# Six layers of windowed attention on one core: another root, half of the normalisation on POOL, and the block transposes moved up

## The chip, the cores and the metric

The kernel runs on one core of one Trainium2 chip. The time is device microseconds from start to end. Three runs of the kernel before took 4267.52, 4268.81 and 4270.26 us; their median is 4268.81 us.

## The reference

The input is 8 batches of 512 tokens of width 128. It is normalised, and two branches take it: one full attention with 16 heads over each batch, and a stack of six layers of windowed attention and feed-forward. Their sum is added to the input. The change touches only the windowed attention of the six layers:

```python
def attn_layer(x, Wqkv, qs, ksc, Wo):
    q, k, v = split(x @ Wqkv)            # 16 heads of 64
    q = l2norm(q) * qs                   # t / max(norm(t), 1e-12)
    k = l2norm(k) * ksc
    q = q * cos * scale + rotate_half(q) * sin * scale
    k = k * cos / scale + rotate_half(k) * sin / scale
    out = local_attention(q, k, v)       # windows of 32: own and previous, softmax(8 q k)
    return out @ Wo
for i in range(6):
    x = attn_layer(shift_tokens(x), ...) + x
    x = ffn_layer(shift_tokens(x), ...) + x
```

## The kernel before, in words

There is no scheduler. Every engine has its own program, the order in it is the order in which the code is written, and engines wait for one another by semaphores. The full attention comes first; from about 1060 us on the layers run, and they are all that the change touches.

The layers go in **turns**. A turn handles one block of 128 tokens; four turns (c = 0 to 3) make a batch, eight batches a layer, so there are 192 turns with attention work, or 48 groups of four. The turns are pipelined over five stages: in one turn, TensorE projects the block that is four stages ahead, VectorE rotates the one three ahead, the scores of the one two ahead are computed, the softmax of the next one is finished, and the output of the present one is added to x. So one turn contains one of each of these on each engine, in this order:

- **DVE** (`turn` at L940): row sums of the exponentials `den` (L945) and reciprocal (L947), which wait for ACT's exponential; rotation of q, three multiplications with the tables (L897, L899), and the same for k; the sums of squares `ss` (L957), the maximum with a floor (L959), and a guess of the root by integer arithmetic (L961); in c = 0 the statistics of the feed-forward (L907 to L917); the addition to x (L968); the 32x32 block transposes `pT` (L972); a feed-forward gate (L924) or, in c = 1, a feed-forward addition (L980); the row maximum of the scores (L991) and their subtraction (L994); at last `qn`, rotated q and k times the root (L1001).
- **POOL**: softmax weights `pn` (L610), which wait for the reciprocal; the addition that ends the rotation of q (L614) and of k (L616); three steps of Newton's method for the root, four small instructions each (`newton`, L399); in c = 0 the same for the feed-forward with its normalisation (L625, L629).
- **ACT**: square of q (L722), copy of the transposed queries `qT` out of PSUM (L726), square of k (L729), copies of the transposed keys (L732, L733), gelu (L714), copy of `xT` (L749), the two copies of `y` (L706), the exponential (L759).
- **PE**: 8 transposes of q and 8 of k (L1042), the products with the output weights (L1254), feed-forward products, the transposed block (L1290), mask and scores (L1302, L1307), the **window products** (L1193), the projections of q and k (L1036).

Queries and keys have sums of squares for 32 heads in one tile `ss`, and one tile `rn` of roots. q is transposed into PSUM banks 0 and 1, k into banks 4 and 5. The products of L1254 go to bank 0 (`ps_o`), so they wait for the copy `qT`. The window products write banks 4, 5, 0 and 1; before them PE waits for `pT`, for the addition to x (which frees bank 0), for the copied keys and for `xT`:

```python
pe.wait_ge(l_pT, t + 2)
pe.wait_ge(l_xw[u], (s.l * NB + s.b + (2 if c == 3 else 1)) * 16)
past(pe, l_x, t + 1)
...
windows_times(u, (pool2, pool0)).then_inc(l_y, 1)
```

ACT's `y` copies wait for the window products, the exponential stands behind them in ACT's queue, and DVE's `den` of the next turn waits for the exponential.

Of the kernel before, what the change touches and what calls it, by code (L numbers as in the profile page):

```python
# [12 lines left out]
P = 128  # L13
# [25 lines left out]
NEG = -1e30  # L39
ROOT_CONSTS = (3.0, 12.0, 768.0)  # L40
ROOT_SCALE = 8192.0
RS = 11
RS_POOL = 12
STEPS = PAIRS * NU
NB_ = 8
# [42 lines left out]
def build(nc, x_in, consts, a_logit, a_bout, a_wqk, a_wv, a_wo, l_wqk, l_wv, l_wo, l_scale, l_w1, l_w2, l_small, out, xd, accd, vd):  # L88
# [8 lines left out]
    with ExitStack() as ctx:  # L97
# [44 lines left out]
        c15 = sb("c15", [P, 2 * H])  # L142
        root_const = sb("root_const", [P, len(ROOT_CONSTS), 2 * H])
        floor_const = sb("floor_const", [P, 2 * H])
        rn = sb("rn", [P, 2 * H])
        rt = sb("rt", [P, 2 * H])
# [84 lines left out]
        l_fl = sem("l_fl")  # L231
        l_gs = sem("l_gs")
        l_rs = sem("l_rs")
# [54 lines left out]
        l_rotk = sem("l_rotk")  # L288
        l_qn = sem("l_qn")
        l_tq = sem("l_tq")  # L290
        l_tk = sem("l_tk")
# [96 lines left out]

        def newton(pool, done, count, root, half, tmp, steps=range(RS_POOL), scaled=False):

            for step in steps:
                const = root_const[:, step // 4] if scaled else c15[:, 0:root.shape[-1]]
                to, a, b, op = ((tmp, root, root, ALU.mult), (tmp, tmp, half, ALU.mult),
                                (tmp, const, tmp, ALU.subtract), (root, root, tmp, ALU.mult))[step % 4]
                if step:
                    pool.wait_ge(done, count * RS_POOL + step)
                nc.gpsimd.tensor_tensor(to, a, b, op).then_inc(done, 1)  # L399

        block = ctx.enter_context(nc.Block())
# [150 lines left out]
        def _(pool):  # L552
            nc.gpsimd.memset(zero[:], 0.0).then_inc(s_zero, 1)
            nc.gpsimd.memset(c15[:], 1.5).then_inc(s_avg, 1)
            for k, value in enumerate(ROOT_CONSTS):
                nc.gpsimd.memset(root_const[:, k], value).then_inc(s_avg, 1)
            nc.gpsimd.memset(floor_const[:], NORM_FLOOR).then_inc(s_avg, 1)
            nc.gpsimd.memset(ones, 1.0).then_inc(s_avg, 1)
            pool.wait_ge(s_avg, 3 + len(ROOT_CONSTS))

# [44 lines left out]
            def turn(s):  # L605
# [6 lines left out]
                if s.has(3):  # L612
                    pool.wait_ge(l_rq, t + 4)
                    nc.gpsimd.tensor_tensor(t1[:, 0:INNER], t1[:, 0:INNER], t2[:, 0:INNER], ALU.add).then_inc(l_rotq, 1)  # L614
                    pool.wait_ge(l_rk, t + 4)
                    nc.gpsimd.tensor_tensor(t1[:, INNER:2 * INNER], t1[:, INNER:2 * INNER], t2[:, INNER:2 * INNER],  # L616
                                            ALU.add).then_inc(l_rotk, 1)
                    pool.wait_ge(l_gs, t + 4)
                    newton(pool, l_rs, t + 3, rn[:], ss[:], rt[:], scaled=True)
                if c == 0 and s.ffn(1):  # L620
# [15 lines left out]
        def _(act):  # L636
# [80 lines left out]
            def turn(s):  # L717
# [5 lines left out]
                if s.has(2):  # L723
                    act.wait_ge(l_tq, t + 3)
                    past(act, l_s, t + 2)
                    act.activation(qT[:].rearrange("p h c -> p (h c)"), pool0, ACT.Copy).then_inc(l_qT, 1)  # L726
                if s.has(3):
# [38 lines left out]
        def _(dve):  # L766
# [174 lines left out]
            def turn(s):  # L941
# [27 lines left out]
                if s.has(1):  # L969
                    dve.wait_ge(l_p, t + 2)  # L970
                    past(dve, l_y, t + 1)
                    nc.vector.transpose(pT[:].rearrange("p n h q -> p n h q"),  # L972
                                        pn[:].rearrange("p (h n k) -> p n h k", h=H, n=2)).then_inc(l_pT, 1)
                if c == 0 and s.ffn(2):
# [31 lines left out]
            dve.wait_ge(s_avg, 3 + len(ROOT_CONSTS))  # L1006
            layers(dve, turn)


        @block.tensor  # L1010
        def _(pe):
# [27 lines left out]

            def transposes(i, pool, src):  # L1040
                for a in range(PAIRS):
                    t = nc.tensor.transpose(pool[:, a * P:(a + 1) * P], src[:, i * INNER + a * P:i * INNER + (a + 1) * P], ident)  # L1042
                return t
# [190 lines left out]
            def turn(s):  # L1234
                c, t = s.c, s.t
                part = fold_part(s)
                if s.has(2):
                    pe.wait_ge(l_qn, t + 3)
                    past(pe, l_y1sb, t + 1)
                    if s.has(3):  # L1240
                        past(pe, l_xT, t + 4)
                    transposes(0, pool0, qn[:]).then_inc(l_tq, 1)
                    past(pe, l_y0sb, t + 1)
                    transposes(1, pool2, qn[:]).then_inc(l_tk, 1)
                if s.has(0):
# [10 lines left out]
                if part is not None:  # L1256
                    n, v, q = part
                    if s.has(2):
                        pe.wait_ge(l_qT, t + 3)
                    past(pe, l_xT, t + 4)  # L1260
                    fold(n, q)
                if s.turn_of(1, 1):
                    pe.wait_ge(l_qT, t + 3)
                    ffn_bias(s.l)
# [15 lines left out]
                if s.has(4):  # L1280
                    pe.wait_ge(l_xs[c], (s.l * NB + s.b + 2) * 16)
                    if s.has(2):
                        pe.wait_ge(l_qT, t + 3)
                    past(pe, l_xT, t + 4)
# [6 lines left out]
                if s.has(2):  # L1291
# [4 lines left out]
                    else:  # L1296
                        past(pe, l_sub, t + 2)
                    pe.wait_ge(l_qT, t + 3)
                    pe.wait_ge(l_kT, t + 3)
# [132 lines left out]
```

## Time and profile before

| | us |
|---|---|
| median of three runs | 4268.81 |
| the profiled execution | 4268.13 |
| its span | 4266.1 |
| PE busy | 3952.3 (93%) |
| DVE busy | 3893.6 (91%) |
| POOL busy | 2675.2 (63%) |
| ACT busy | 2604.4 (61%) |

The span is what lies between the first and the last instruction of the profile; some 2 us lie around it. Busy shares are means over stages: the full attention up to about 1060 us, the layers up to about 4200 us, and an end of some 66 us in which the pipeline drains. In the rows further down, a line of the timeline gives the start, the duration, the engine, the line of the code, the operation, output and inputs, and in brackets how long the engine stood idle before it and who ended that.

### The profile page before, as it was taken

What the parts mean: (1) busy time and instruction counts of PE and PEld (TensorE: products, weight loads), DVE (VectorE), ACT (ScalarE), POOL (GpSimd) and SP (SyncE); (2) the same over time, 40 slices, a digit from 0 to 9 for tenths busy, and PEclk for the clock granted to TensorE, in tenths of its full rate; (3) what the DMA queues carried; (4) which work ended last, traced back from release to release, by engine and by line L of the source; (5) the groups of instructions that cost most, each with busy time, mean ns of one, the idle gap of its engine ahead of it and who ended that gap; (6) DMA issues with size and microseconds to landing.
All of it is one profiled execution on the core that took longest, in us unless ns stands there. A gap on an engine that the chain in (4) does not pass through costs nothing. (4 is left out here: it accounts for less than half of the span.)

```text
span 4266.1 us, 124858 instructions
## 1 busy us (share of the span) xinstructions
PE 3952.3 (93%) x48616; PEld 2743.1 (64%) x48616; DVE 3893.6 (91%) x4860; ACT 2604.4 (61%) x3780; POOL 2675.2 (63%) x4692
## 2 busy tenths in 40 slices
PE   7999999996899999999999999999999999999996
PEld 4666666664666666666666666666666666666664
DVE  6888888886999999999999999999999999999994
ACT  4555565563566666666666666666666666666663
POOL 5555555554676766767667676666766767667673
PEclk9999999998999999999999999999999999999999
DMA  5444444441000011000110001100011000010000
GB/s 134 92 92 94 94 94 91 91 93 45 23 16 17 16 30 29 16 17 16 30 29 16 17 16 30 30 16 17 16 29 29 16 17 16 20 38 16 18 15 14
DMA packets 342439, 165.07 MB, mean 39 GB/s; under 512 B 114240, under 2 KB 337472, under 8 KB 341184
## 3 DMA queue, kind: packets, MB, share of 16 engines
q1 hardware_dynamic: 342208, 161.99, 17.1%
q8 instruction: 145, 2.38, 0.2%
q14 instruction: 86, 0.70, 0.1%
HBM read 115.67 MB, written 33.69 MB: 35 GB/s over the span
## 5 line engine op out<-in xcount | busy, mean ns | idle before, releaser
L610 POOL TENSOR_TENSOR pn<-es,rden 128x1024 f32<-128x1024 f32 x192 | 366.3, 1908 | 693.6 <-DVE rden L947 693.6
L706 ACT ACTIVATE y<-ps 128x1024 f32<-128x1024 f32 x384 | 372.2, 1021 | 510.2 <-PE ps L1193 510.2
L614 POOL TENSOR_TENSOR t<-t 128x1024 f32<-128x1024 f32 x192 | 454.3, 2366 | 88.0 <-DVE t L899 88.0
L658 ACT ACTIVATE t<-ps,amx 128x512 f32<-128x512 f32 x512 | 347.6, 688 | 250.9 <-DVE amx L805 250.9
L899 DVE TENSOR_TENSOR t<-ps,tabl 128x512 f32<-128x512 f32 x768 | 490.8, 681 | 0.0
L897 DVE TENSOR_TENSOR t<-ps,tabl 128x1024 f32<-128x1024 f32 x384 | 467.0, 1216 | 16.7 <-ACT sq L722 11.4
L616 POOL TENSOR_TENSOR t<-t 128x1024 f32<-128x1024 f32 x192 | 452.6, 2357 | 3.6 <-DVE t L899 3.6
L1001 DVE TENSOR_TENSOR qn<-t,rn 128x2048 f32<-128x2048 f32 x192 | 438.1, 2282 | 5.1 <-POOL rn L399 5.1
L957 DVE TENSOR_REDUCE ss<-sq 128x32 f32<-128x2048 f32 x192 | 436.9, 2275 | 0.0
L805 DVE TENSOR_REDUCE amx<-ps 128x2 f32<-128x1024 f32 x256 | 310.9, 1215 | 129.5 <-PE ps L1064 129.5
L1042 PEld LDWEIGHTS ps<-cst,qn 128*128 128x128 f32 x3072 | 349.3, 141 | 116.0 <-issue 59.9
L1254 PE MATMUL ps<-acc,y 128*128 128x128 f32 x3072 | 367.9, 278 | 36.9 <-ACT qT L726 32.6
L1254 PE MATMUL ps<-wm,y 128*128 128x128 f32 x3072 | 365.7, 277 | 33.8 <-ACT qT L726 33.8
L1254 PEld LDWEIGHTS ps<-acc,y 128*128 128x128 f32 x3072 | 352.5, 193 | 58.0 <-issue 57.9
L1307 PE MATMUL ps<-kpad,qT 128*32 128x128 f32 x12288 | 385.5, 279 | 0.0
L1254 PEld LDWEIGHTS ps<-wm,y 128*128 128x128 f32 x3072 | 350.2, 192 | 53.9 <-issue 53.9
L1042 PE MATMUL ps<-cst,qn 128*128 128x128 f32 x3072 | 370.0, 274 | 13.1 <-DVE qn L1001 10.3
L1036 PE MATMUL ps<-wm,xT 128*128 128x512 f32 x768 | 357.9, 609 | 8.8 <-ACT xT L749 8.8
L1307 PEld LDWEIGHTS ps<-kpad,qT 128*32 128x32 f32 x12288 | 332.0, 112 | 45.6 <-issue 44.2
L1036 PE MATMUL ps<-acc,xT 128*128 128x512 f32 x768 | 355.2, 605 | 0.0
L813 DVE STREAM_TRANSPOSE kpad<-t 128x1024 f32<-128x1024 f32 x256 | 315.4, 1232 | 0.0
L1064 PE MATMUL ps<-qk 64*128 64x512 f32 x1024 | 291.4, 646 | 4.3 <-ACT t L658 3.5
(134 smaller groups left out, 8234.2 us busy)
## 6 DMA issues: line engine op xcount, KB each, us to landing
wm<-values_dram SPq DMA_DIRECT2D x128, 256.0 KB, 5.2
y<-values_dram SPq DMA_DIRECT2D x128, 256.0 KB, 4.9
values_dram<-qT SPq DMA_DIRECT2D x64, 256.0 KB, 2.3
tokens_dram<-x SPq DMA_DIRECT2D x96, 128.0 KB
xs<-tokens_dram SPq DMA_DIRECT2D x192, 64.0 KB, 1.8
xw<-tokens_dram SPq DMA_DIRECT2D x192, 64.0 KB, 1.9
xsh<-x SPq DMA_DIRECT2D x48, 128.0 KB
xsh<-x SPq DMA_DIRECT2D x48, 127.0 KB
```

Source lines behind the costliest of these rows:

```text
L610: nc.gpsimd.tensor_tensor(heads(pn[:], H), heads(es[:], H), rden[:].unsqueeze(2).to_broadcast([P, H, KEYS]), ALU.mult).then_inc(l_p, 1)
L614: nc.gpsimd.tensor_tensor(t1[:, 0:INNER], t1[:, 0:INNER], t2[:, 0:INNER], ALU.add).then_inc(l_rotq, 1)
L616: nc.gpsimd.tensor_tensor(t1[:, INNER:2 * INNER], t1[:, INNER:2 * INNER], t2[:, INNER:2 * INNER], ALU.add).then_inc(l_rotk, 1)
L706: return act.activation(y[:].rearrange("p h (w q) -> p w h q", w=NW)[:, 2 * half:2 * half + 2], src.rearrange("p (w h q) -> p w h q", w=2, ...
L897: nc.vector.tensor_tensor(t13, q3, tabl[:, 0, u, i].unsqueeze(1).to_broadcast([P, H, DH]), ALU.mult)
L899: sine = nc.vector.tensor_tensor(t23[:, :, lo:lo + DH // 2], q3[:, :, hi:hi + DH // 2], tabl[:, 1, u, i, lo:lo + DH // 2].unsqueeze(1).to_ ...
L957: nc.vector.tensor_reduce(ss[:], heads(sq[:], 2 * H), X, ALU.add).then_inc(l_ss, 1)
L1001: nc.vector.tensor_tensor(heads(qn[:], 2 * H), heads(t1, 2 * H), rn[:].unsqueeze(2).to_broadcast([P, 2 * H, DH]), ALU.mult).then_inc(l_qn, 1)
L1036: m = nc.tensor.matmul(pool[:, s * 512:(s + 1) * 512], src, wqkL[v][:, i * INNER + s * 512:i * INNER + (s + 1) * 512], start=True, stop=True)
L1042: t = nc.tensor.transpose(pool[:, a * P:(a + 1) * P], src[:, i * INNER + a * P:i * INNER + (a + 1) * P], ident)
L1254: m = nc.tensor.matmul(ps_o, y[:, h], mhL[s.v][:, slot(h)], start=(h == 0), stop=(h == H - 1))
L1307: m = nc.tensor.matmul(pool1[w * WIN:(w + 1) * WIN, a * 2 * KEYS:(a + 1) * 2 * KEYS], qT[:, a, w * WIN:(w + 1) * WIN], kpad[:, 2 * a:2 * a ...
```

## The change

In each turn of the layers:

1. The root. The guess on DVE (L961) and the three Newton steps on POOL are replaced by one instruction of POOL that raises the floored sum of squares to the power -0.5, and one Newton step of four instructions behind it (`polish`), all on 128x32 elements. The constants follow: the tables are now divided by 2, not by 8192.
2. The normalisation. DVE multiplies only the query half by its root (128x1024 in place of 128x2048); the key half is a POOL instruction, behind the root in POOL's queue, with a semaphore `l_kn` of its own, for which PE's transposes of k wait.
3. The query copy. PE signals the transposes of q in two halves, one for each PSUM bank, and ACT copies them in two instructions of 128x512; PE's output products wait for the first, what comes later for the second.
4. The order on DVE. The block transposes `pT` stand ahead of the sums of squares, and no longer behind the addition to x.

```diff
-ROOT_CONSTS = (3.0, 12.0, 768.0)
-ROOT_SCALE = 8192.0
+ROOT_CONST = 3.0
+ROOT_SCALE = 2.0
...
+        def polish(pool, done, count, root, square, const, tmp):
+            nc.gpsimd.tensor_tensor(root, square, power_const[:, 0:root.shape[-1]], ALU.pow).then_inc(done, 1)
+            pool.wait_ge(done, count * RS_STEP + 1)
+            nc.gpsimd.tensor_tensor(tmp, root, root, ALU.mult).then_inc(done, 1)
+            pool.wait_ge(done, count * RS_STEP + 2)
+            nc.gpsimd.tensor_tensor(tmp, tmp, square, ALU.mult).then_inc(done, 1)
+            pool.wait_ge(done, count * RS_STEP + 3)
+            nc.gpsimd.tensor_tensor(tmp, const, tmp, ALU.subtract).then_inc(done, 1)
+            pool.wait_ge(done, count * RS_STEP + 4)
+            nc.gpsimd.tensor_tensor(root, root, tmp, ALU.mult).then_inc(done, 1)
...
@@ POOL, turn
-                    pool.wait_ge(l_gs, t + 4)
-                    newton(pool, l_rs, t + 3, rn[:], ss[:], rt[:], scaled=True)
+                    pool.wait_ge(l_fl, t + 4)
+                    polish(pool, l_rs, t + 3, rn[:], ss[:], root_const[:], rt[:])
+                if s.has(3):
+                    pool.wait_ge(l_rotk, t + 4)
+                    pool.wait_ge(l_rs, (t + 4) * RS_STEP)
+                    past(pool, l_tk, t + 3)
+                    nc.gpsimd.tensor_tensor(heads(qn[:, INNER:2 * INNER], H), heads(t1[:, INNER:2 * INNER], H),
+                                            rn[:, H:2 * H].unsqueeze(2).to_broadcast([P, H, DH]), ALU.mult).then_inc(l_kn, 1)
@@ ACT, turn
-                    act.wait_ge(l_tq, t + 3)
                     past(act, l_s, t + 2)
-                    act.activation(qT[:].rearrange("p h c -> p (h c)"), pool0, ACT.Copy).then_inc(l_qT, 1)
+                    for half in range(2):
+                        act.wait_ge(l_tq, 2 * t + 5 + half)
+                        act.activation(qT[:, 4 * half:4 * half + 4].rearrange("p h c -> p (h c)"), bank(half),
+                                       ACT.Copy).then_inc(l_qT, 1)
@@ DVE, turn
+                    past(dve, l_kn, t + 3)
                     rotate(1, u, pool1, l_rk)
+                if s.has(1):
+                    dve.wait_ge(l_p, t + 2)
+                    past(dve, l_y, t + 1)
+                    nc.vector.transpose(pT[:].rearrange("p n h q -> p n h q"),
+                                        pn[:].rearrange("p (h n k) -> p n h k", h=H, n=2)).then_inc(l_pT, 1)
+                if s.has(3):
                     nc.vector.tensor_reduce(ss[:], heads(sq[:], 2 * H), X, ALU.add).then_inc(l_ss, 1)
                     dve.wait_ge(l_ss, t + 4)
                     nc.vector.tensor_tensor(ss[:], ss[:], floor_const[:], ALU.max).then_inc(l_fl, 1)
-                    dve.wait_ge(l_fl, t + 4)
-                    nc.vector.tensor_scalar(rn[:].bitcast(I32), ss[:].bitcast(I32), -0.5, float(0x5F3759DF),
-                                            ALU.mult, ALU.add).then_inc(l_gs, 1)
...
-                    dve.wait_ge(l_rs, (t + 4) * RS_POOL)
+                    dve.wait_ge(l_rs, (t + 4) * RS_STEP)
                     dve.wait_ge(l_rotq, t + 4)
-                    dve.wait_ge(l_rotk, t + 4)
-                    past(dve, l_tk, t + 3)
-                    nc.vector.tensor_tensor(heads(qn[:], 2 * H), heads(t1, 2 * H),
-                                            rn[:].unsqueeze(2).to_broadcast([P, 2 * H, DH]), ALU.mult).then_inc(l_qn, 1)
+                    past(dve, l_tq, 2 * t + 6)
+                    nc.vector.tensor_tensor(heads(qn[:, 0:INNER], H), heads(t1[:, 0:INNER], H),
+                                            rn[:, 0:H].unsqueeze(2).to_broadcast([P, H, DH]), ALU.mult).then_inc(l_qn, 1)
@@ PE, turn
-                    transposes(0, pool0, qn[:]).then_inc(l_tq, 1)
+                    for half in range(2):
+                        transposes(0, pool0, qn[:], half).then_inc(l_tq, 1)
+                    pe.wait_ge(l_kn, t + 3)
                     past(pe, l_y0sb, t + 1)
                     transposes(1, pool2, qn[:]).then_inc(l_tk, 1)
...
-                        pe.wait_ge(l_qT, t + 3)
+                        pe.wait_ge(l_qT, 2 * t + 5)
```

DVE before, one turn (c = 2) from `den` to the gate; the line numbers are those of each kernel:

```order
L945 TENSOR_REDUCE den<-es 128x16
L947 RECIPROCAL rden<-den 128x16
L897 TENSOR_TENSOR t<-ps,tabl 128x1024
L899 TENSOR_TENSOR t<-ps,tabl 128x16x32 x2
L897 TENSOR_TENSOR t<-ps,tabl 128x1024
L899 TENSOR_TENSOR t<-ps,tabl 128x16x32 x2
L957 TENSOR_REDUCE ss<-sq 128x32
L959 TENSOR_TENSOR ss<-ss,floor_const 128x32
L961 TENSOR_SCALAR rn<-ss 128x32
L968 TENSOR_TENSOR x<-x,ps 128x128
L972 STREAM_TRANSPOSE pT<-pn 128x1024
L924 SCALAR_TENSOR_TENSOR fh<-ps,b1s,qk 128x512
```

DVE now, the same turn:

```order
L967 TENSOR_REDUCE den<-es 128x16
L969 RECIPROCAL rden<-den 128x16
L919 TENSOR_TENSOR t<-ps,tabl 128x1024
L921 TENSOR_TENSOR t<-ps,tabl 128x16x32 x2
L919 TENSOR_TENSOR t<-ps,tabl 128x1024
L921 TENSOR_TENSOR t<-ps,tabl 128x16x32 x2
L983 STREAM_TRANSPOSE pT<-pn 128x1024
L986 TENSOR_REDUCE ss<-sq 128x32
L988 TENSOR_TENSOR ss<-ss,floor_const 128x32
L994 TENSOR_TENSOR x<-x,ps 128x128
L946 SCALAR_TENSOR_TENSOR fh<-ps,b1s,qk 128x512
```

`pT` has moved up past the sums, the floor and the addition to x; the guess is gone; the addition to x is now the last of the two things of DVE that the window products wait for.

POOL before, from the key rotation on (`rn` is the root, `rt` its temporary); eleven more such small instructions follow the first one shown, eight of them left out here:

```order
L616 TENSOR_TENSOR t<-t 128x1024
L399 TENSOR_TENSOR rt<-rn 128x32
L398 ISA
L399 TENSOR_TENSOR rt<-rt,ss 128x32
L398 REGISTER_ALU
L399 TENSOR_TENSOR rt<-root_const,rt 128x32
L398 REGISTER_ALU
L399 TENSOR_TENSOR rn<-rn,rt 128x32
L398 REGISTER_ALU
```

POOL now, the same place:

```order
L630 TENSOR_TENSOR t<-t 128x1024
L405 TENSOR_TENSOR rn<-ss,power_const 128x32
L406 REGISTER_ALU
L407 TENSOR_TENSOR rt<-rn 128x32
L408 REGISTER_ALU
L409 TENSOR_TENSOR rt<-rt,ss 128x32
L410 REGISTER_ALU
L411 TENSOR_TENSOR rt<-root_const,rt 128x32
L412 REGISTER_ALU
L413 TENSOR_TENSOR rn<-rn,rt 128x32
L636 REGISTER_ALU
L638 TENSOR_TENSOR qn<-t,rn 128x1024
```

Five small instructions stand where twelve stood, and the key half of `qn` has come in behind them.

## Rows read from the trace of the kernel before

**Rows 1.** Busy time by engine over the layers (span, then busy, clock, DMA).

```profile
1060.00:4200.00 3140.00, 2965.47 (x28343) 2056.47 (x28342) 3031.95 (x3774) 1999.21 (x2318) 2112.52 (x3493) 1.00 0.08 21
```

**Rows 2.** Waits over 1095 to 4200 us: total, times, longest.

```profile
PE ps L1193 <- DVE pT L972: 73.8, 54, 1.7
PE ps L1254 <- ACT qT L726: 65.3, 186, 0.5
```

**Rows 3.** Timeline of PE: window products of c=0 and c=1, turn c=2, next c=0.

```profile
2998.04 1.14 PE L1193 MATMUL ps<-pT,xw 32*128 32x512 f32 x8 [1.74 <-DVE pT L972]
...
3014.92 1.14 PE L1193 MATMUL ps<-pT,xw 32*128 32x512 f32 x8
...
3020.39 1.91 PE L1042 MATMUL ps<-cst,qn 128*128 128x128 f32 x16
3022.64 3.81 PE L1254 MATMUL ps<-acc,y 128*128 128x128 f32 x32 [0.33 <-ACT qT L726]
...
3030.41 1.14 PE L1193 MATMUL ps<-pT,xw 32*128 32x512 f32 x8
...
3063.20 1.14 PE L1193 MATMUL ps<-pT,xw 32*128 32x512 f32 x8 [1.68 <-DVE pT L972]
```

**Rows 4.** Timeline of ACT in turn c=2, and its 512-wide copy in c=1.

```profile
3010.03 0.60 ACT L743 ACTIVATE qk<-ps 128x512 f32<-128x512 f32 x1 [1.58 <-PE ps L1202]
...
3016.99 1.94 ACT L706 ACTIVATE y<-ps 128x1024 f32<-128x1024 f32 x2 [3.89 <-PE ps L1193]
3018.81 1.06 ACT L759 ACTIVATE es<-es 128x1024 f32<-128x1024 f32 x1
```

**Rows 5.** Timeline of DVE in turn c=2, to the next turn's `den`.

```profile
3019.91 1.22 DVE L945 TENSOR_REDUCE den<-es 128x16 f32<-128x1024 f32 x1 [0.16 <-ACT es L759]
...
3026.00 2.27 DVE L957 TENSOR_REDUCE ss<-sq 128x32 f32<-128x2048 f32 x1
3028.30 0.27 DVE L959 TENSOR_TENSOR ss<-ss,floor_const 128x32 f32<-128x32 f32 x1
3028.61 0.18 DVE L961 TENSOR_SCALAR rn<-ss 128x32 int32<-128x32 int32 x1
3028.74 0.29 DVE L968 TENSOR_TENSOR x<-x,ps 128x128 f32 x1
3028.94 1.24 DVE L972 STREAM_TRANSPOSE pT<-pn 128x1024 f32<-128x1024 f32 x1
...
3033.12 2.28 DVE L1001 TENSOR_TENSOR qn<-t,rn 128x2048 f32<-128x2048 f32 x1
3035.39 1.22 DVE L945 TENSOR_REDUCE den<-es 128x16 f32<-128x1024 f32 x1
```

**Rows 6.** Timeline of DVE in turn c=0: the statistics and the transposes.

```profile
3059.69 0.87 DVE L907 BATCH_NORM_STATS2 st<-xsh 128x6 f32<-128x128 f32 x4
...
3061.63 1.24 DVE L972 STREAM_TRANSPOSE pT<-pn 128x1024 f32<-128x1024 f32 x1
```

**Rows 7.** Timeline of POOL in turn c=2: weights, key rotation, first and last Newton instruction.

```profile
3021.49 1.90 POOL L610 TENSOR_TENSOR pn<-es,rden 128x1024 f32<-128x1024 f32 x1 [4.84 <-DVE rden L947]
...
3026.16 2.37 POOL L616 TENSOR_TENSOR t<-t 128x1024 f32<-128x1024 f32 x1
3028.87 0.24 POOL L399 TENSOR_TENSOR rt<-rn 128x32 f32<-128x32 f32 x1 [0.34 <-DVE rn L961]
...
3032.46 0.25 POOL L399 TENSOR_TENSOR rn<-rn,rt 128x32 f32<-128x32 f32 x1
```

**Rows 8.** Timeline of DVE: the floor in c=1, the normalisation in c=0.

```profile
3011.50 1.01 DVE L959 TENSOR_TENSOR ss<-ss,floor_const 128x32 f32<-128x32 f32 x1
...
3065.81 2.28 DVE L1001 TENSOR_TENSOR qn<-t,rn 128x2048 f32<-128x2048 f32 x1
```

**Rows 9.** Timeline of POOL, same places: key rotation, and a feed-forward Newton instruction.

```profile
3010.10 2.36 POOL L616 TENSOR_TENSOR t<-t 128x1024 f32<-128x1024 f32 x1
...
3065.86 2.28 POOL L399 TENSOR_TENSOR frt<-frn 128x4 f32<-128x4 f32 x1
```

More of the change, by code:

```diff
@@ L39 @@
 NEG = -1e30
-ROOT_CONSTS = (3.0, 12.0, 768.0)
-ROOT_SCALE = 8192.0
+ROOT_CONST = 3.0
+ROOT_SCALE = 2.0
 RS = 11
 RS_POOL = 12
+RS_STEP = 5
 STEPS = PAIRS * NU
@@ L142, in build @@
         c15 = sb("c15", [P, 2 * H])
-        root_const = sb("root_const", [P, len(ROOT_CONSTS), 2 * H])
+        root_const = sb("root_const", [P, 2 * H])
         floor_const = sb("floor_const", [P, 2 * H])
+        power_const = sb("power_const", [P, 2 * H])
         rn = sb("rn", [P, 2 * H])
@@ L231, in build @@
         l_fl = sem("l_fl")
-        l_gs = sem("l_gs")
         l_rs = sem("l_rs")
@@ L289, in build @@
         l_qn = sem("l_qn")
+        l_kn = sem("l_kn")
         l_tq = sem("l_tq")
@@ L387, in heads, with newton @@
             return ap.rearrange("p (h d) -> p h d", h=n)
-        def newton(pool, done, count, root, half, tmp, steps=range(RS_POOL), scaled=False):
+        def newton(pool, done, count, root, half, tmp, steps=range(RS_POOL)):
             for step in steps:
-                const = root_const[:, step // 4] if scaled else c15[:, 0:root.shape[-1]]
                 to, a, b, op = ((tmp, root, root, ALU.mult), (tmp, tmp, half, ALU.mult),
-                                (tmp, const, tmp, ALU.subtract), (root, root, tmp, ALU.mult))[step % 4]
+                                (tmp, c15[:, 0:root.shape[-1]], tmp, ALU.subtract), (root, root, tmp, ALU.mult))[step % 4]
                 if step:
@@ L554, in _ @@
             nc.gpsimd.memset(c15[:], 1.5).then_inc(s_avg, 1)
-            for k, value in enumerate(ROOT_CONSTS):
-                nc.gpsimd.memset(root_const[:, k], value).then_inc(s_avg, 1)
+            nc.gpsimd.memset(root_const[:], ROOT_CONST).then_inc(s_avg, 1)
             nc.gpsimd.memset(floor_const[:], NORM_FLOOR).then_inc(s_avg, 1)
+            nc.gpsimd.memset(power_const[:], -0.5).then_inc(s_avg, 1)
             nc.gpsimd.memset(ones, 1.0).then_inc(s_avg, 1)
-            pool.wait_ge(s_avg, 3 + len(ROOT_CONSTS))
+            pool.wait_ge(s_avg, 5)
             def copy_batch(b):
@@ L968, in turn @@
                     nc.vector.tensor_tensor(xb, xb, ps_o, ALU.add).then_inc(l_x, 1)
[L969 to L973, printed above, removed]
                 if c == 0 and s.ffn(2):
@@ L996, in turn @@
                 if s.has(3):
-                    dve.wait_ge(l_rs, (t + 4) * RS_POOL)
+                    dve.wait_ge(l_rs, (t + 4) * RS_STEP)
                     dve.wait_ge(l_rotq, t + 4)
-                    dve.wait_ge(l_rotk, t + 4)
-                    past(dve, l_tk, t + 3)
-                    nc.vector.tensor_tensor(heads(qn[:], 2 * H), heads(t1, 2 * H),
-                                            rn[:].unsqueeze(2).to_broadcast([P, 2 * H, DH]), ALU.mult).then_inc(l_qn, 1)
+                    past(dve, l_tq, 2 * t + 6)
+                    nc.vector.tensor_tensor(heads(qn[:, 0:INNER], H), heads(t1[:, 0:INNER], H),
+                                            rn[:, 0:H].unsqueeze(2).to_broadcast([P, H, DH]), ALU.mult).then_inc(l_qn, 1)
             dve.wait_ge(s_tb, 16)
             scale_tables(0)
-            dve.wait_ge(s_avg, 3 + len(ROOT_CONSTS))
+            dve.wait_ge(s_avg, 5)
             layers(dve, turn)
@@ L1038, in project, with transposes @@
                 return m
-            def transposes(i, pool, src):
-                for a in range(PAIRS):
+            def transposes(i, pool, src, half=None):
+                for a in range(PAIRS) if half is None else range(half * 4, half * 4 + 4):
                     t = nc.tensor.transpose(pool[:, a * P:(a + 1) * P], src[:, i * INNER + a * P:i * INNER + (a + 1) * P], ident)
@@ L1258, in turn @@
                     if s.has(2):
-                        pe.wait_ge(l_qT, t + 3)
+                        pe.wait_ge(l_qT, 2 * t + 6)
                     past(pe, l_xT, t + 4)
@@ L1262, in turn @@
                 if s.turn_of(1, 1):
-                    pe.wait_ge(l_qT, t + 3)
+                    pe.wait_ge(l_qT, 2 * t + 6)
                     ffn_bias(s.l)
@@ L1282, in turn @@
                     if s.has(2):
-                        pe.wait_ge(l_qT, t + 3)
+                        pe.wait_ge(l_qT, 2 * t + 6)
                     past(pe, l_xT, t + 4)
@@ L1297, in turn @@
                         past(pe, l_sub, t + 2)
-                    pe.wait_ge(l_qT, t + 3)
+                    pe.wait_ge(l_qT, 2 * t + 6)
                     pe.wait_ge(l_kT, t + 3)
```

## The prediction

> **What bounds the kernel now.** I read the busy table first. Over the layers PE is busy 2965 of 3140 us (94%) and DVE 3032 (97%), POOL 2113 and ACT 1999 [rows 1]. Two engines are nearly full, so shares alone don't say what a lighter DVE is worth; the order of waits within a turn must. The waits view is short: PE waits 74 us for the block transposes, 54 times, and 65 us for the query copy, 186 times at 0.35 [rows 2].
>
> Then I followed one group of four turns in the timeline. I call the start of the window products W. From W of one c=0 turn to W of the next, 3063.20 - 2998.04 = 65.16 us [rows 3]; 48 groups make 3128 us, which is the layers' 3140. Single turns: c=1 takes 16.88, c=2 15.49 [rows 3], c=3 (no row, the same instructions as c=2) 15.5, and c=0 the rest, 17.3.
>
> Three chains have nearly one length there. *PE's own*: in c=1 and c=2 it has only the 0.33 us before L1254 to spare, in c=0 also the 1.68 for the transposes [rows 3]. *DVE's own*: its rows of c=2 stand back to back, from `den` at 3019.91 to `den` at 3035.39, 15.48 us [rows 5]. *The ring through all engines*: W at 3014.92, the copies of y at 3016.99, the exponential to 3019.87, `den` at 3019.91 (0.16 idle, released by the exponential), and along DVE to the end of pT at 3030.18, then W at 3030.41 [rows 3 to 5]. Shortening DVE alone therefore leaves the ring: W to `den` is 4.99 us of PE and ACT that the change doesn't touch.
>
> **The change part by part.**
>
> *Half of `qn` leaves DVE.* 2.28 us for 2048 elements become about 1.2 for 1024 (half, plus some start; the half-sized rows on DVE, such as `den`, have 1.22) [rows 5]. DVE loses 1.1 us a turn. In the ring this is worth nothing: the end of `qn` and the end of the exponential release `den` at the same moment now (3035.40 and the 0.04 behind the exponential), so DVE will stand 1.1 us waiting for the exponential instead. 192 turns take some 200 us off DVE's busy time and leave the end where it is.
>
> *The guess goes.* From the floor to the next instruction there are 28.74 - 28.30 = 0.44 us in c=2, of which the guess with its wait is 0.18 to 0.31 [rows 5]; I take the lower, its own duration. This lies in the ring, in every turn.
>
> *The transposes move up.* pT starts 2.9 us earlier. But the window products wait for the addition to x too, and this now stands behind the sums, the floor and (in c=0) the statistics, where pT stood. DVE has the same work between `den` and the later of the two: in c=2 the last releaser ended at 3030.18 [rows 5] and will end at 3030.18 - 0.18 = 3030.00. What ends last has another name; the time is that of the guess. The hand-over from DVE to W was 0.33 us in c=0, where PE stood waiting (61.63 + 1.24 = 62.87, then 63.20) [rows 3, 6]; behind an addition it could be none or the same 0.35. I take 0.2, since part of the waits that follow pT's in PE's program is then already past. So W of c=2 comes at 3030.20 in place of 3030.41, 0.21 earlier; c=3 the same; c=0 at 62.87 - 0.18 + 0.2 = 62.89 in place of 63.20, 0.31 earlier. The hand-over's ends, 0 and 0.35, make each of the three 0.2 better or 0.15 worse.
>
> *The query copy by banks.* L1254 starts 2.25 us behind the transposes' start, and these take 1.91 [rows 3]: 0.33 of wait. In future the first bank is transposed after 0.5 us, its copy takes about 0.60 [rows 4], and is there before the transposes of k are through. In c=1, where PE is the longest chain, 0.33 come off: W to W 16.55. DVE's ring in c=1 is 15.3, so it doesn't hold this back. In the other turns PE's own chain becomes 15.15, just below the ring. ACT pays 0.17 a turn for two starts instead of one; it has idle time in each turn, and its next piece, the square of k, starts no later.
>
> *The root.* Of twelve instructions from 3028.87 to 3032.71, 0.33 apart [rows 7], five are left: p for the power and 4 x 0.33 = 1.3. No row shows a power on POOL. Its nearest row is a multiplication of the same shape, 0.24 [rows 7]; the other end is the dearest instruction that POOL has here, 2.36 [rows 9], and beyond it the whole old chain, 3.8. I take 0.25 to 0.85, near the first, because up to 0.85 it makes no difference, as follows. The Trainium skill (GPSIMD Engine Reference, section "Performance versus the Vector engine") gives a cost of about 12 cycles an element for branches on the data; for 32 elements at the page's 1.2 GHz that is an estimate of 0.32 us on top of the multiplication's time. No run here shows it.
>
> *The key half on POOL.* The form is that of `pn`, 1.90 [rows 7]; POOL is idle 4.84 us in front of the next `pn`, and the root gets 2.5 us shorter less p. In c=2 the addition to x now ends at 3030.0 and begins at 3029.7, where the floor ends; the power starts 0.1 later, the root is ready at 3031.1 + p and the key product runs from 3031.2 + p to 3033.1 + p. PE's transposes of k need it at 3036.6: free. But DVE wants to start the query half at 3033.12 - 0.18 = 3032.94, and here is a cover to look at. Two rows show that DVE and POOL exclude each other in instructions with two inputs from SBUF: the floor in c=1 took 1.01 us in place of 0.27 and ended as the key rotation ended (3012.51 and 3012.46), and a POOL instruction of 0.20 took 2.28 beside `qn` [rows 8, 9]. So the query half waits for the key half, until 3033.1 + p, and `den` can follow 1.2 later, at 3034.3 + p. The exponential lets it start at 3035.18: there are 0.85 us of cover for p. In c=1 turns the sums are done 1.2 us earlier relative to W, in c=0 turns the root has the 1.74 us of the statistics; only the intervals behind c=2 and c=3 are exposed. The feed-forward's root in c=0, behind it on POOL, starts some 0.9 + p later but is held by a `qn` half as long; it stays within 0.5 us of where it was, and `pn` with it.
> The Trainium skill (SBUF — State Buffer, section "Who interferes with whom") says the same of such pairs: whichever starts first keeps the shared read port for its whole instruction and the other blocks. The trace agrees, with the 2.28 for 0.20.
>
> *Sum.* 0.33 (c=1) + 0.21 + 0.21 + 0.31 = 1.06 us a group, 48 groups: 51 us. From the profiled execution's 4268.1 that gives 4217; the median of the runs is 0.7 above it, within their spread. With the hand-over's ends, 3 x 0.2 or 3 x 0.15 x 48, own range 4190 to 4240.
>
> **The rivals.**
>
> *B, PE becomes the only bound.* If the early pT freed the window products, PE would lose all four 0.33 and the 1.68: 65.16 - 3.0 = 62.2 a group, 144 us, 4124. For it speaks that the waits view names pT alone. Against it: the addition to x is a wait of the same instruction, and DVE reaches it no earlier.
>
> *C, a middling power.* For p between 0.85 and 1.7 the key half is in front of the query half each time, and the two exposed turns of a group lose p - 0.85 each: 96 us for each us. At p = 1.3 that is 43 of the 51 us back, 4260.
>
> *D, slower: POOL holds the read port in front of the query half.* The same place, with the point of decision p = 0.85 + 51/96 = 1.4. At p = 2.36 [rows 9] c=2 and c=3 lose 1.5 each, c=1's early sums no longer suffice (0.35), and `pn` with both rotations come late enough in c=1 to hold the floor (0.3): 3.65 lost, 1.06 won, 124 us, 4392. For it: a power is more than a multiplication, and POOL is the slower engine for the same shape already (2.36 for an addition of 128x1024 [rows 9], where DVE takes half of 2.28 for a product of that size). Against it: nothing in the trace; only that the query half could win the start from p = 1.7 on, since both wait for the same root. Then nearly all of the gain stays, 4230.
>
> *E, no change.* If the addition's hand-over is 0.35 and the guess was hidden by PE's own 15.15 plus new waits (for the key half, between the transposes), c=2 and c=3 give nothing and c=0 and c=1 little: 4262 to 4275.
>
> **How the numbers follow.** Forecast 0.53; B 0.04; C 0.17, of which 0.10 is still faster by over 0.2% (9 us, about what a measurement of this kernel can tell from no change), 0.03 within it and 0.04 slower; D 0.18, with 0.03 in the branch that stays faster and 0.15 slower; E 0.08, 0.05 within 0.2% and 0.03 slower. Faster 0.70, same 0.08, slower 0.22. The range goes from the forecast's own lower end, 4190, up to 4290, where p is 1.6; outside lie B and most of D.
>
> **What would show it.** Right: DVE's busy time falls to about 3620 us, with an idle of about 1 us in front of `den` for the exponential; W follows the addition to x, not pT; PE has no wait left before L1254's successor; a group of four turns takes 64.1 us, with 15.3 in c=2 and c=3, 17.0 in c=0 and 16.55 in c=1; the power takes under 0.85. Wrong: a query half that starts when the key half ends and pushes `den` past the exponential (C, D), or a PE without idle in c=0 (B).

## The result, and the profile after

The changed kernel takes 4915.24 us (median of four runs, 4910.09 to 4917.95) where the kernel before took 4268.17 in the same comparison: a ratio of 1.151, 95% interval 1.149 to 1.153. The prediction said 4217, with a range of 4190 to 4290. It had the wrong sign.

The page of the changed kernel names the reason in its first group: the power on POOL takes 5.44 us, 192 times. That is 1044 us of POOL's time. Its line:

```profile
L405 POOL TENSOR_TENSOR rn<-ss,power_const 128x32 f32<-128x32 f32 x192 | 1044.4, 5440 | 176.0 <-DVE ss L988 169.9
```

The waits from 1100 to 4800 us (total, times, longest) answer to [rows 2]:

```profile
DVE qn L1021 <- POOL rn L413: 495.6, 179, 4.3
PE ps L1062 <- DVE qn L1021: 477.9, 174, 4.0
...
DVE pT L983 <- POOL pn L624: 54.3, 42, 3.0
...
PE ps L1213 <- DVE x L994: 46.0, 48, 1.5
```

In this stretch DVE waits for the root 179 times, and PE waits for DVE's query half 174 times. DVE's `den` waited for ACT's exponential in only 7 of the 192 turns, 7.6 us together, so neither PE nor ACT stands in the chain that now sets the turn. The query copy is no longer among PE's waits, and the window products wait for the addition to x where they waited for pT. The busy row over the layers, the answer to [rows 1], has PE at 84%, DVE at 81% and POOL at 82%: none of them is full. DVE and POOL wait for each other in turn, and PE waits for DVE. The mean granted clock of TensorE over this stretch is 0.94, where it was 1.00:

```profile
1100.00:4840.00 3740.00, 3132.39 (x28030) 2203.14 (x28029) 3044.88 (x3556) 2013.77 (x2486) 3051.99 (x2328) 0.94 0.07 17
```

One turn (c = 2) on DVE, the answer to [rows 5]:

```profile
3501.66 1.21 DVE L967 TENSOR_REDUCE den<-es 128x16 f32<-128x1024 f32 x1
...
3507.74 1.24 DVE L983 STREAM_TRANSPOSE pT<-pn 128x1024 f32<-128x1024 f32 x1
3508.90 2.24 DVE L986 TENSOR_REDUCE ss<-sq 128x32 f32<-128x2048 f32 x1
3511.18 0.19 DVE L988 TENSOR_TENSOR ss<-ss,floor_const 128x32 f32<-128x32 f32 x1
3511.31 0.29 DVE L994 TENSOR_TENSOR x<-x,ps 128x128 f32 x1
...
3514.06 1.23 DVE L1015 TENSOR_TENSOR es<-ps,mx 128x1024 f32<-128x1024 f32 x1
3518.34 2.92 DVE L1021 TENSOR_TENSOR qn<-t,rn 128x1024 f32<-128x1024 f32 x1 [3.06 <-POOL rn L413]
3521.18 1.21 DVE L967 TENSOR_REDUCE den<-es 128x16 f32<-128x1024 f32 x1
```

and on POOL, the answer to [rows 7]:

```profile
3511.45 5.44 POOL L405 TENSOR_TENSOR rn<-ss,power_const 128x32 f32<-128x32 f32 x1 [1.18 <-DVE ss L988]
3516.97 0.24 POOL L407 TENSOR_TENSOR rt<-rn 128x32 f32<-128x32 f32 x1
...
3517.95 0.25 POOL L413 TENSOR_TENSOR rn<-rn,rt 128x32 f32<-128x32 f32 x1
3518.28 1.90 POOL L638 TENSOR_TENSOR qn<-t,rn 128x1024 f32<-128x1024 f32 x1
```

Read the two together and the turn closes on itself: 9.71 us from `den` to the end of the floor, 5.60 for the power with its hand-overs, 1.31 for the polishing, 1.90 in which POOL has the key half and DVE's query half, issued 0.06 later, is blocked, and 1.00 until `den` starts again. That is 19.52 us, where the turn took 15.48 [rows 5]. The query half alone takes 1.22 us (a run below shows it); here it shows as 2.92, because the time in which it is blocked counts as its own.

POOL is not always the first. In 22 of the 192 turns DVE started 0.10 us ahead, and there it is the key half on POOL that is blocked:

```profile
1687.03 1.23 DVE L1021 TENSOR_TENSOR qn<-t,rn 128x1024 f32<-128x1024 f32 x1 [3.35 <-POOL rn L413]
1687.12 2.89 POOL L638 TENSOR_TENSOR qn<-t,rn 128x1024 f32<-128x1024 f32 x1
```

This turn (c=3, with the same work as the one above) took 17.65 us where the others take 19.52, and so did nearly all of the 22. In 164 turns POOL was ahead by 0.05 to 0.08 us; what decides between the two was not found. In the last 6, all c=1, DVE reached its half 0.6 to 1.9 us behind POOL.

The turn c=1 takes 2.26 us more than c=2. The feed-forward work of POOL stands between the key half of c=0 and the softmax weights of c=1, so the transposes wait for the weights, and the key rotation, late by as much, holds DVE's floor for 1.02 us:

```profile
3487.19 1.25 DVE L983 STREAM_TRANSPOSE pT<-pn 128x1024 f32<-128x1024 f32 x1 [1.14 <-POOL pn L624]
...
3490.64 1.21 DVE L988 TENSOR_TENSOR ss<-ss,floor_const 128x32 f32<-128x32 f32 x1
```

The starts of `den` in all 192 turns give the account by turn (median us from one `den` to the next; the last column is the mean over all 191 intervals):

| kernel | c=0 | c=1 | c=2 | c=3 | mean |
|---|---|---|---|---|---|
| before | 17.38 | 16.81 | 15.48 | 15.48 | 16.59 |
| after | 19.54 | 21.78 | 19.52 | 19.52 | 19.95 |
| after, multiplication for the power | 16.84 | 16.24 | 15.27 | 15.27 | 16.15 |
| after, key half behind | 17.83 | 22.22 | 17.81 | 17.81 | 19.02 |
| after, transposes back | 18.47 | 21.58 | 18.45 | 18.45 | 19.10 |
| the best version below | 15.99 | 16.58 | 15.24 | 14.92 | 15.96 |

191 intervals times 3.36 are 642 us; the medians of the runs differ by 647. So nearly the whole loss lies in the turns.

PE's part, the answer to [rows 3]:

```profile
3501.80 3.33 PE L1062 MATMUL ps<-cst,qn 128*128 128x128 f32 x16 [3.59 <-DVE qn L1021]
3504.96 3.74 PE L1276 MATMUL ps<-acc,y 128*128 128x128 f32 x32
...
3512.66 1.14 PE L1213 MATMUL ps<-pT,xw 32*128 32x512 f32 x8
```

The sixteen transposes take 3.33 us where they took 1.91. PE had just stood 3.59 us, and the granted clock was at the lower of its two levels, 1.2 of 2.4 GHz, while they ran:

```profile
3501.50:3504.50 3.00, 2.70 (x13) 2.71 (x14) 2.96 (x5) 1.29 (x3) 1.26 (x1) 0.50 0.00 0
```

This is a consequence and no further cause in these turns: DVE had the scores, had subtracted their maximum and still stood 3.06 us before it got its root.

### The profile page after: what moved, and what is told of

Read it like the earlier page. It is cut to its first block and busy times, and to the rows that moved or that the text cites. A ratio compares the mean times of both kernels' runs of the same rounds, so it can differ in the third digit from the quotient of the medians.

```text
span 4913.3 us, 123751 instructions
## 1 busy us (share of the span) xinstructions
PE 4155.9 (85%) x48616; PEld 2915.8 (59%) x48616; DVE 3927.9 (80%) x4668; ACT 2637.6 (54%) x3972; POOL 3671.7 (75%) x3539
## 5 line engine op out<-in xcount | busy, mean ns | idle before, releaser
L405 POOL TENSOR_TENSOR rn<-ss,power_const 128x32 f32<-128x32 f32 x192 | 1044.4, 5440 | 176.0 <-DVE ss L988 169.9
L1062 PE MATMUL ps<-cst,qn 128*128 128x128 f32 x3072 | 511.7, 335 | 516.1 <-DVE qn L1021 504.5
L1021 DVE TENSOR_TENSOR qn<-t,rn 128x1024 f32<-128x1024 f32 x192 | 516.7, 2691 | 523.9 <-POOL rn L413 523.9
L1062 PEld LDWEIGHTS ps<-cst,qn 128*128 128x128 f32 x3072 | 448.4, 174 | 677.3 <-DVE qn L1021 504.6
L747 ACT ACTIVATE qT<-ps 128x512 f32<-128x512 f32 x384 | 217.0, 596 | 626.1 <-PE ps L1062 625.4
L638 POOL TENSOR_TENSOR qn<-t,rn 128x1024 f32<-128x1024 f32 x192 | 386.8, 2015 | 16.3
L1276 PE MATMUL ps<-acc,y 128*128 128x128 f32 x3072 | 390.8, 290 | 4.3 <-ACT y L726 4.3
L1276 PE MATMUL ps<-wm,y 128*128 128x128 f32 x3072 | 390.9, 290 | 0.0
L1276 PEld LDWEIGHTS ps<-acc,y 128*128 128x128 f32 x3072 | 386.9, 208 | 5.9 <-issue 5.9
L1276 PEld LDWEIGHTS ps<-wm,y 128*128 128x128 f32 x3072 | 387.2, 208 | 0.0
```

Source lines behind the costliest of these rows:

```text
L405: nc.gpsimd.tensor_tensor(root, square, power_const[:, 0:root.shape[-1]], ALU.pow).then_inc(done, 1)
L638: nc.gpsimd.tensor_tensor(heads(qn[:, INNER:2 * INNER], H), heads(t1[:, INNER:2 * INNER], H), rn[:, H:2 * H].unsqueeze(2).to_broadcast([P, ...
L1021: nc.vector.tensor_tensor(heads(qn[:, 0:INNER], H), heads(t1[:, 0:INNER], H), rn[:, 0:H].unsqueeze(2).to_broadcast([P, H, DH]), ALU.mult). ...
L1276: m = nc.tensor.matmul(ps_o, y[:, h], mhL[s.v][:, slot(h)], start=(h == 0), stop=(h == H - 1))
```

## The experiments

All are compared with the kernel before on the same chip. The kernel before took 4268.2 to 4269.9 us there (median by chip), so a difference between two of the experiments, or to the changed kernel's 4915.24, is good to 1 or 2 us. Theory P says that the power stands in a ring of DVE and POOL; what else could have made 647 us (the order, the two halves that exclude each other, the clock) is told apart by the first four, which start from the changed kernel.

**A multiplication in place of the power.**

```diff
-            nc.gpsimd.tensor_tensor(root, square, power_const[:, 0:root.shape[-1]], ALU.pow).then_inc(done, 1)
+            nc.gpsimd.tensor_tensor(root, square, power_const[:, 0:root.shape[-1]], ALU.mult).then_inc(done, 1)
```

> The changed kernel with a multiplication of the same shape in the place of the power (what is left out: the power, so the root's value). Theory P (the power of 5.44 us stands in a ring of DVE and POOL, from the row sums over the sums of squares, the root and the normalisation back to the row sums): 5.2 us of it go, the ring falls below the ring through the window products, and the time is the one forecast for a cheap power, 4217 us (4190 to 4240). Rival Q (what costs is the rest: the order, the two halves of the normalisation that exclude each other, TensorE's lower clock): the time stays above 4500 us.

Measured: 4177.99 us, ratio 0.979 (0.977 to 0.980). With one instruction exchanged, 737 us go and the kernel is faster than before, as theory P says; rival Q is out. The time is 39 us below the sum for a cheap power, and 12 below the interval that the theory gave; where from is told in the next section. Its rows:

```profile
3035.70 0.19 DVE L988 TENSOR_TENSOR ss<-ss,floor_const 128x32 f32<-128x32 f32 x1
3035.83 0.29 DVE L994 TENSOR_TENSOR x<-x,ps 128x128 f32 x1
...
3039.09 1.50 DVE L1021 TENSOR_TENSOR qn<-t,rn 128x1024 f32<-128x1024 f32 x1
3041.44 1.22 DVE L967 TENSOR_REDUCE den<-es 128x16 f32<-128x1024 f32 x1 [0.85 <-ACT es L781]
```

```profile
3036.47 1.14 PE L1213 MATMUL ps<-pT,xw 32*128 32x512 f32 x8 [0.29 <-DVE x L994]
```

This is the machine that the prediction described: DVE stands 0.85 us for the exponential, the query half is held 0.3 us by the key half, and the window products wait for the addition to x, 0.35 us behind its end.

**The old root in the changed kernel.** The guess and three Newton steps come back, the rest of the change stays.

```diff
-                    polish(pool, l_rs, t + 3, rn[:], ss[:], root_const[:], rt[:])
+                    newton(pool, l_rs, t + 3, rn[:], ss[:], rt[:], scaled=True)
```

> The changed kernel with the old root (guess on DVE, three Newton steps on POOL) and everything else of the change. Theory P: the root takes 0.3 + 3.9 us; the ring of DVE and POOL is 9.8 (row sums to floor) + 4.2 + 1.9 (key half) + 1.1 (query half) = 17.0 us in all four turns of a group, 68 against 65.2 before: 4400 us (4360 to 4440). Rival: Newton's steps are hidden as they were before, and the time is 4210 to 4240.

Measured: 4435.52 us, ratio 1.039 (1.037 to 1.041), within the theory's interval. By turns it is less exact: c=0, c=2 and c=3 take 16.8 to 17.1 us, c=1 18.9, where 17.0 was said for all four. So the other three parts of the change together lose 166 us with Newton's root of some 4 us, and gain 92 with the multiplication's 1.6. The power takes more than either.

**The key half behind the query half.**

```diff
                     past(pool, l_tk, t + 3)
+                    pool.wait_ge(l_qn, t + 4)
```

> The changed kernel with one wait more: POOL starts the key half of the normalisation only when DVE has ended the query half. Theory P with the shared port: the query half starts at once when the root is ready, takes 1.2 instead of 2.9 us, and each turn's ring is 1.7 to 1.8 us shorter: 4580 to 4670 us. Rival: the query half is slow for another reason, or the key half is what TensorE waits for; the time stays within 40 us of 4915.

Measured: 4737.81 us, ratio 1.110 (1.108 to 1.112): 177 us better than the changed kernel, but not the 245 to 335 expected. The turns say which part of the expectation failed. c=0, c=2 and c=3 take 17.8 us, 1.7 less, as worked out; the mechanism of the shared port is confirmed. There was less to win than in every turn, though: 22 turns of the changed kernel had the query half in front already. And c=1 takes 22.2, 0.4 more: the feed-forward work on POOL stands behind the key half, so the softmax weights come late and the transposes wait for them:

```profile
3524.11 1.25 DVE L984 STREAM_TRANSPOSE pT<-pn 128x1024 f32<-128x1024 f32 x1 [3.29 <-POOL pn L624]
```

**The transposes back behind the addition to x.** The two blocks change places again in DVE's program, nothing else.

> The changed kernel with the block transposes back behind the addition to x. Theory P: the sums, and with them the power, start 1.16 us earlier in every turn's ring, 4 x 48 x 1.16 = 223 us: 4690 us (4670 to 4760). Rival (the early transposes are what the window products need): 4915 or more.

Measured: 4748.88 us, ratio 1.112 (1.110 to 1.114), 166 us better than the changed kernel, within the interval, where 223 was the value. c=0, c=2 and c=3 take 18.46, 1.07 less; c=1 takes 0.20 less. Where the root is late, what is put ahead of the sums of squares lengthens these three turns by nearly its own duration.

**The new root alone, on the kernel before.** The edit is the one of the change; normalisation, copy and order stay old.

> The kernel before with the new root alone (power and one polishing step); normalisation whole on DVE, old copy, old order. Theory P: den to floor 8.7, power and polishing 0.1 + 6.8, normalisation 2.2: a ring of 17.9 us in place of 15.5 in c=2 and c=3, 17.9 for 17.3 in c=0, about 1 us more in c=1: 6.4 x 48 = 307, 4575 us (4500 to 4650). Rival Q (the power hurts only together with the early transposes and the halves): under 4350.

Measured: 4643.39 us, ratio 1.088 (1.086 to 1.090). The power costs 374 us without any help from the other parts, at the upper end of what was expected. c=2 and c=3 take 17.7 us, as worked out; c=1 takes 20.6, 3.8 more than before, where 1 more was expected.

**The query copy by banks alone, on the kernel before.**

> The kernel before with the query copy by banks alone. Theory: only c=1 has TensorE as its longest chain; it wins 0.33 us, or 0.56 as in the run with the multiplication (16.32 for 16.88), 48 times: 4241 to 4253 us. Rival: all 186 waits of 0.35 us count, 65 us, 4205; or none counts, 4268.

Measured: 4252.67 us, ratio 0.996 (0.995 to 0.998): 17 us, the theory's value for a gain of 0.33 in c=1. The turns don't bear that value out: the median c=1 is 0.56 shorter and c=2 and c=3 are 0.08 shorter, while the mean c=0 is 0.43 longer, which stays unexplained. PE's waits show why the 65 us of [rows 2] did not all come back; the wait moved to the transposes of the window products, from 54 times to 129:

```profile
PE ps L1198 <- DVE pT L977: 133.5, 129, 2.4
```

**The early transposes alone, on the kernel before.**

> The kernel before with the block transposes ahead of the sums of squares, alone. Theory: the window products are released no earlier (they wait for the addition to x as well), and the root is ready 1.16 us later, of which 0.35 are covered, so c=2 and c=3 lose 0.8 us each: 77 us, 4330 to 4350. Rival: the transposes were the limit, as the waits view says; 73 us are won, 4195.

Measured: 4303.07 us, ratio 1.008 (1.007 to 1.009): slower, by 33 us where 60 to 80 were expected. The sign and the mechanism hold: in c=2 and c=3 `qn` now waits for the root and the turn takes 16.1 us. The size was off: c=2 and c=3 lost 0.61 each where 0.8 was said, and c=0, where the statistics give the root time, got 0.33 shorter; c=1 got 0.33 longer.

```profile
3054.04 2.29 DVE L1002 TENSOR_TENSOR qn<-t,rn 128x2048 f32<-128x2048 f32 x1 [0.66 <-POOL rn L399]
```

**The key half on POOL alone, on the kernel before.**

> The kernel before with the key half of the normalisation on POOL alone. Theory: the root is ready 12.9 us behind the row sums in c=2 and c=3, the key half is first and holds the query half until 14.8, the row sums follow at 16.0 in place of 15.5; in c=0 the statistics leave time for both: 0.5 x 2 x 48 = 48 us lost, 4310 to 4330. Rival: the DVE time that is saved (1.1 us a turn) counts, 4230 or less.

Measured: 4309.62 us, ratio 1.009 (1.008 to 1.011), at the edge of the interval. Taking 1.1 us a turn from a DVE that was 97% busy makes the kernel slower: in c=1, c=2 and c=3 the half that left blocks the half that stayed, which takes 2.7 us for 1.22. The turns c=2 and c=3 lose 0.29, where 0.5 was said, and c=1 loses 0.67, where nothing was.

**The power in two halves.**

```diff
+            for part in (slice(0, H), slice(H, 2 * H)):
+                nc.gpsimd.tensor_tensor(root[:, part], square[:, part], power_const[:, part], ALU.pow).then_inc(done, 1)
```

> The changed kernel with the power issued as two instructions of 128x16 in place of one of 128x32, to see whether its 5.44 us are paid by the element or by the instruction. Theory: by the element, about 0.16 us each; each half takes 2.7 to 2.9 us, and the time rises by some 0.2 us a turn, to 4940 to 4960. Rival: by the instruction (a fixed cost); each half takes about 5.2 us and the turn grows by 5 us, 5800.

Measured: 4977.82 us, ratio 1.166 (1.164 to 1.168), 18 us above the interval for the time; the durations are as expected (nanoseconds, least, median, greatest):

```profile
L406 POOL TENSOR_TENSOR rn<-ss,power_const x364: 2903/2910/2917, 1104.9 to 4794.6; 128x16 f32<-128x16 f32 x182
```

Two of 2.91 against one of 5.44: the difference of 16 columns is 2.53, so by these two sizes a column of 128 costs 0.158 us, and the start 0.38. The power is paid by the element.

**The best version.** The guess on DVE and Newton on POOL with two steps in place of three, the key half on POOL behind the query half except in c=0, the copy by banks, and both the transposes and the addition to x ahead of the sums of squares.

```diff
-ROOT_CONSTS = (3.0, 12.0, 768.0)
-ROOT_SCALE = 8192.0
+ROOT_CONSTS = (3.0, 12.0)
+ROOT_SCALE = 16.0
...
@@ POOL, ahead of the key half
+                    if c != 0:
+                        pool.wait_ge(l_qn, t + 4)
@@ DVE, turn
                     nc.vector.transpose(pT[:]...).then_inc(l_pT, 1)
+                if s.has(0):
+                    dve.wait_ge(l_o, t + 1)
+                    nc.vector.tensor_tensor(xb, xb, ps_o, ALU.add).then_inc(l_x, 1)
+                if s.has(3):
                     nc.vector.tensor_reduce(ss[:], heads(sq[:], 2 * H), X, ALU.add).then_inc(l_ss, 1)
```

> A version from the findings: guess on DVE and two Newton steps on POOL (one step fewer than before), the key half on POOL but behind the query half except in c=0, the copy by banks, and both the transposes and the addition to x ahead of the sums of squares. Theory: both things that the window products wait for are then early, the root is ready at 13.0 us behind the row sums, just when the query half wants it, and TensorE's own chain is what remains: 15.05 x 3 + 16.32 = 61.5 us a group for 65.2, 4092 us (4080 to 4150). Rival: POOL's feed-forward work between c=0 and c=1 and the shared port hold DVE, and it stays at the 4178 us of the run with the multiplication or above.

Measured: 4144.40 us, ratio 0.971 (0.970 to 0.972): faster than both kernels. Here PE goes from one turn to the next without a wait:

```profile
3011.10 1.14 PE L1207 MATMUL ps<-pT,xw 32*128 32x512 f32 x8
...
3016.57 1.91 PE L1056 MATMUL ps<-cst,qn 128*128 128x128 f32 x16
3018.32 3.74 PE L1270 MATMUL ps<-acc,y 128*128 128x128 f32 x32
...
3026.02 1.14 PE L1207 MATMUL ps<-pT,xw 32*128 32x512 f32 x8
```

14.92 us is PE's own chain. The time lies in the interval, 52 us above its value of 4092. The larger part is c=0, 16.0 us for the 15.05 said: there PE waits for DVE's subtraction, by up to 0.6 us a turn and 18 us together. c=1 takes 16.6 for 16.32, and c=2 15.24.

**The same with three Newton steps.** One step more of 1.3 us; nothing else differs.

> The best version with the three Newton steps of before in place of two. Theory: the root comes 1.3 us later; in the version with two steps DVE stands 0.5 to 0.8 us before the row sums, and 0.4 before that the root was ready, so about 0.1 to 0.4 us a turn is left over in c=2 and c=3: 4150 to 4185 us. Rival: the whole 1.3 us counts in each turn, 4395.

Measured: 4281.74 us, ratio 1.003 (1.002 to 1.004). The expectation, 4150 to 4185, is wrong: 1.3 us of latency cost 137 us, 0.7 a turn. It counted the slack of DVE only. In c=2 and c=3, which lose 0.58 and 0.43, the key half stands behind the query half, and PE waits for it:

```profile
3026.74 1.09 PE L1056 MATMUL ps<-cst,qn 128*128 128x128 f32 x8 [0.19 <-DVE qn L1015]
3028.81 1.09 PE L1056 MATMUL ps<-cst,qn 128*128 128x128 f32 x8 [0.98 <-POOL qn L629]
```

In c=0, which loses 1.08, POOL is the first, by 0.62 us where it was 1.95, and the query half is blocked: 2.36 us for 1.22. The 0.83 of c=1 was not taken apart.

**The multiplication with the early addition to x.** The first experiment's kernel (the power is left out) with the order of the best version.

> The changed kernel with a multiplication in the place of the power (the power is left out) and the addition to x moved up behind the block transposes, ahead of the sums of squares. Theory: in the run with the multiplication the window products waited 0.3 us for the addition in c=2 and c=3 and 1.8 in c=0; both go, TensorE's chain of 15.0, 15.0, 15.0 and 16.3 remains, 61.4 for 63.6 us a group: 4178 - 105 = 4073 (4070 to 4120). Rival: the transposes alone were the limit, and nothing changes from 4178.

Measured: 4105.51 us, ratio 0.962 (0.960 to 0.963): 72 us less than with the transposes alone. The theory's value was 4073 (4070 to 4120). So the addition to x was what held the window products, as the prediction read from the code.

## Why the prediction was wrong

**The root: this is the step that failed.** "I take 0.25 to 0.85, near the first, because up to 0.85 it makes no difference." It measured 5.44 us. No row of the trace before showed a power on POOL, and the value was taken from a multiplication of the same shape, 0.24. The two ends named were also too low: "2.36, and beyond it the whole old chain, 3.8". A cost that nothing shows was set beside the operation that looks like it in the code, not beside what it does. By the Trainium skill (GPSIMD Engine Reference, section "Performance versus the Vector engine"), with its 12 cycles an element for branching, the estimate was 0.32 us more, some 0.6 in all; that misses by nearly as much, and no run here shows whether the power branches.

**The rival D was the right mechanism, with the right price.** It put the point of decision at p = 1.4 and priced each us of p beyond 0.85 at 1 us in c=2 and c=3. With p = 5.44 that gives 15.27 + 4.6 = 19.9 a turn; measured 19.52. Its other branch, in which the query half wins the start, is there too, in 22 turns, most of which took 17.65 us. But D got 0.18 of the chances at an assumed p of 2.36. It also took c=0 and c=1 as nearly covered, which at this length they are not: 19.5 and 21.8, that is 2.7 and 5.5 more than with the multiplication. The sharper point is that one unknown decided everything, and the forecast was given for the cheap half of it.

**The key half in front of the query half: right.** 2.92 us in place of 1.22, and putting it behind took 1.7 us from three turns of four. The Trainium skill's rule (SBUF — State Buffer, section "Who interferes with whom"), that the first to start keeps the port and the other blocks, holds here in both directions: where POOL started 0.06 us earlier, DVE's instruction ended 1.08 us behind POOL's; where DVE started 0.10 us earlier, DVE's took 1.23 us and POOL's 2.89 for 1.90.

**Half of `qn` off DVE is worth nothing: right.** With the multiplication DVE stands 0.85 to 1.2 us before `den`; DVE's busy time is 3632 us, where "about 3620" was said.

**The window products wait for the addition to x: right**, shown by the waits and by the run that moves the addition (72 us).

**The terms of the sum, for a root that is cheap.** Said 51 us, measured 4268 - 4178 = 90 to 92. Even where a term came out, it was partly luck. c=2 and c=3 have 0.22 where 0.21 was said, but by two errors that cancel: DVE ends the last thing that the window products wait for 0.32 us sooner behind `den`, not 0.18 (of the two values for the guess, 0.18 and 0.31, the upper was right), and the hand-over from DVE to the window products was 0.35, not 0.2, where it had been 0.24 without an idle time of PE. c=0 has 0.54 for 0.31: there the hand-over was the 0.2 that was said (0.19, it had been 0.33), and DVE is 0.41 sooner. c=1 has 0.57 for 0.33: the transposes' start and that of L1254's products lay 2.25 us apart and now lie 1.75, since without the wait PE's next product starts while the modelled end of the last transpose still runs; so the 0.33 of wait was not the whole distance. That makes 1.55 a group, 74 us. Some 11 more lie in the turns at the start of a layer, which the sum took as all others (the mean of c=1 is 17.67 before and 16.99 with the multiplication, 0.68 apart where the medians are 0.57 apart), and some 5 outside the turns, most of them before the first `den`. What shortens these was not taken apart and stays open.

**The copy by banks: right in size, and in part by luck**: 17 us alone, made up otherwise than the sum has it.

**The range.** It was cut at a p of 1.6 with nothing in the trace that excluded more. The own bounds for the unknown would have reached beyond 4392.

## What to carry to other kernels

Before an operation is exchanged for a shorter list of instructions, measure the new kind of instruction by itself: five instructions took 6.8 us where twelve took 3.8. Where a forecast rests on one unmeasured duration, work out the duration at which the sign turns (here 1.4 us) and give the chances by how sure one is to be under it, not by the value one likes. And an engine's share of busy time is no reason to unload it: taking 1.1 us a turn from a DVE that was 97% busy cost 41 us alone, while moving one 0.29 us addition ahead of a 2.2 us sum won 72 in the kernel with the multiplication, because PE's window products, and ACT's copies and the exponential behind them, waited for it.

## What the runs showed of the hardware

- A power of two tensors on POOL: 5.44 us for 128x32 (5.52 to the start of the next instruction), 2.91 for 128x16. By these two sizes that is 0.158 us a column and 0.38 for the start; a multiplication of 128x32 takes 0.25, one part in 22.
- DVE and POOL instructions with two inputs from SBUF exclude each other even when both wait for the same semaphore, and a start 0.05 to 0.10 us ahead decides. In 164 of the changed kernel's 192 turns POOL was ahead, and DVE's 1.22 us became 2.92; in 22 DVE was, and POOL's 1.90 us became 2.89. The blocked time is part of the instruction's recorded duration.
- After PE had stood 3.6 us the granted clock was 0.50, and sixteen transposes took 3.33 us in place of 1.91; the mean granted clock over the layers was 0.94 in place of 1.00.
